# Recurrence of a one-core kernel: GpSimd computes two of VectorE's fp32 products in every time step

## The reference, cut to what matters

```python
def step(h, xs):
    xzt, xrt, xht = xs
    z = jax.nn.sigmoid(xzt + h @ U_z + vz)
    r = jax.nn.sigmoid(xrt + h @ U_r + vr)
    hh = jnp.tanh(xht + r * h @ U + vh)
    h_new = (1.0 - z) * h + z * hh
    return (h_new, h_new)
h0 = jnp.zeros((seq.shape[0], U.shape[0]), seq.dtype)
_, out_t = jax.lax.scan(step, h0, xs)
```

## Time and profile before

| what | value |
|---|---|
| median of 3 runs | 3793.93 us (3781.72 to 3805.06) |
| profiled execution | 3778.47 us |
| its span, first to last instruction | 3776.7 us |
| PE / DVE / ACT / POOL busy | 3250.4 / 2066.5 / 1501.4 / 628.7 us |
| one instruction of each of the 512 steps (ScalarE's r) | first at 2443.3 us, last at 3494.5 us |

### The profile page before, as it was taken

How to read it: one execution, slowest core, us unless ns; L and a number is a source line. 1 busy time by engine, 2 the same in 40 slices (tenths; PEclk the granted TensorE clock), 3 DMA queues, 4 the chain that set the end, 5 groups by cost and what they waited for, 6 DMA issues and landing times. The chain is left out here.

```text
span 3776.7 us, 109696 instructions
## 1 busy us (share of the span) xinstructions
PE 3250.4 (86%) x44394; PEld 2131.3 (56%) x44394; DVE 2066.5 (55%) x8157; ACT 1501.4 (40%) x4199; POOL 628.7 (17%) x361
## 2 busy tenths in 40 slices
PE   7895865899999876679986678899999999999899
PEld 3322442222333223678863234499999899999566
DVE  6324454555555515663327544377777677777554
ACT  3485541555454531666642222222222222222222
POOL 0000000666666750431110000000000000000000
PEclk8798987999999976899997789855555555555999
DMA  1000003000000005211110000100000000000000
GB/s 69 1 1 12 1 1 111 1 1 1 1 1 1 1 13 173 84 43 37 38 66 33 26 0 0 56 4 4 4 4 4 5 4 4 4 4 4 6 7 10
DMA packets 53379, 79.50 MB, mean 21 GB/s; under 512 B 11878, under 2 KB 43323, under 8 KB 51996
## 3 DMA queue, kind: packets, MB, share of 16 engines
q1 hardware_dynamic: 47504, 61.59, 4.9%
q0 software_dynamic: 3408, 9.34, 0.7%
q10 hardware_dynamic: 1988, 1.77, 0.2%
HBM read 56.01 MB, written 16.67 MB: 19 GB/s over the span
## 5 line engine op out<-in xcount | busy, mean ns | idle before, releaser
L1308 DVE TENSOR_REDUCE diff_mx<-diff_m_ps 128x1 f32<-128x512 f32 x512 | 330.0, 686 | 330.2 <-PE diff_m_ps L1158 330.2
L2756 PE MATMUL gru_sums<-gru_take,gru_u 128*128 128x4 f16 x12288 | 477.5, 167 | 5.5 <-issue 4.7
L2756 PE MATMUL gru_sums<-gru_keep,gru_u 128*128 128x4 f16 x12288 | 471.2, 166 | 4.1 <-DVE gru_keep L2830 2.2
L2756 PEld LDWEIGHTS gru_sums<-gru_take,gru_u 128*128 128x128 f16 x12288 | 430.4, 104 | 5.7 <-issue 4.8
L2756 PEld LDWEIGHTS gru_sums<-gru_keep,gru_u 128*128 128x128 f16 x12288 | 410.6, 104 | 18.3 <-issue 3.8
L1262 ACT ACTIVATE diff_probs<-diff_s_ps 128x512 f32<-128x512 f32 x512 | 277.9, 594 | 222.0 <-PE diff_s_ps L1152 221.9
L1152 PE MATMUL diff_s_ps<-diff_qk 32*128 32x512 f32 x1024 | 292.5, 645 | 63.6 <-DVE diff_mx L1308 56.0
L2756 PE MATMUL gru_sums<-gru_rh,gru_u 128*128 128x4 f16 x6144 | 280.1, 170 | 27.0 <-DVE gru_rh L2825 4.3
L1158 PE MATMUL diff_m_ps<-diff_qk 32*128 32x512 f32 x1024 | 293.6, 650 | 6.4 <-DVE diff_mx L1308 6.4
L1354 POOL TENSOR_TENSOR diff_sums<-diff_sums,diff_probs 128x2048 f32<-128x2048 f32 x64 | 289.4, 4521 | 31.4 <-ACT diff_probs L1262 31.1
L2756 PEld LDWEIGHTS gru_sums<-gru_rh,gru_u 128*128 128x128 f16 x6144 | 237.7, 107 | 69.4 <-DVE gru_rh L2825 6.0
(11 more groups left out here) (485 smaller groups left out, 5578.8 us busy)
## 6 DMA issues: line engine op xcount, KB each, us to landing
moe_weights<-in_L_ffn_W SPq DMA_DIRECT2D x16, 1024.0 KB, 12.8
expert_slots<-diff_blank SPq DMA_DIRECT2D x1, 5031.0 KB, 20.9
stream_a<-expert_slots SPq DMA_DIRECT2D x39, 129.0 KB, 2.1
moe_weights<-in_L_cond_w_R SPq DMA_DIRECT2D x1, 4096.0 KB, 15.4
moe_both<-expert_pairs SPq DMA_DIRECT2D x4, 1024.0 KB, 9.7
stream_b<-in_x SPq DMA_DIRECT2D x4, 512.0 KB, 8.1
hyp_wf<-in_L_cond_w_f SPq DMA_DIRECT2D x2, 1024.0 KB, 8.5
stream_b<-in_xT SPq DMA_DIRECT2D x1, 2048.0 KB, 12.2
```

The source lines that it names most:

```text
L1308: dve.tensor_reduce(mx[:, i % 2, kt, at:at + 1], m_ps[:, m % 3, :], X_AXIS, ALU.max).then_inc(ph.maxes_ready, 1)
L2756: last = pe.matmul(sums[:, par, g, m * B:(m + 1) * B], part[:, g, c, m * P:(m + 1) * P], state[:, c * B:(c + 1) * B], start=False, stop=(l ...
```

## The change

GpSimd gets a loop over the steps. In each it computes the fp32 `rh` = r*h and the fp32 `take` = hh*zs; VectorE no longer does. So that `take` is one plain product, VectorE computes `zs` = z times the scale, between `keep` and `keep2`. VectorE's `rh2` now waits for `rh1` and for `rh`, its `take2` for `take1` and for `take`. GpSimd's copies of the history stand between its products: three of four at the start of a step ahead of that step's `rh`, the fourth at the loop's end.

```diff
--- before.py
+++ after.py
@@ -2624,10 +2624,10 @@
         ph = Phase(nc, ctx, "gru")
         (ph.dve_step, ph.pe_done, ph.act_read, ph.h_ready, ph.r_sums, ph.z_sums, ph.hh_sums, ph.r_ready,
          ph.z_ready, ph.rh1_ready, ph.rh_ready, ph.rh2_ready, ph.keep1_ready, ph.keep_ready, ph.keep2_ready, ph.take1_ready,
-         ph.take_ready, ph.take2_ready, ph.hh_ready, ph.kept, ph.inputs_ready) = ph.semaphores(
+         ph.take_ready, ph.take2_ready, ph.hh_ready, ph.kept, ph.inputs_ready, ph.zs_ready) = ph.semaphores(
             "dve_step", "pe_done", "act_read", "h_ready", "r_sums", "z_sums", "hh_sums", "r_ready",
             "z_ready", "rh1_ready", "rh_ready", "rh2_ready", "keep1_ready", "keep_ready", "keep2_ready", "take1_ready",
-            "take_ready", "take2_ready", "hh_ready", "kept", "inputs_ready")
+            "take_ready", "take2_ready", "hh_ready", "kept", "inputs_ready", "zs_ready")
         N, KEPT, S = DC * B, KEPT_AT_ONCE, STEPS_IN_BODY
         COPIES = S // KEPT
         w, u, cw, bias, condT = early.w, early.u, early.cw, early.bias, early.condT
@@ -2648,6 +2648,7 @@
         r = ph.sb("r", [P, N])
         z = ph.sb("z", [P, N])
         rest = ph.sb("rest", [P, N])
+        zs = ph.sb("zs", [P, N])
         rh = ph.sb("rh", [P, N])
         rh1 = ph.sb("rh1", [P, N], F16)
         rh2 = ph.sb("rh2", [P, N], F16)
@@ -2823,12 +2824,14 @@
                         before = h[:, (s - 1) % S, :]
                         dve.wait_ge(ph.r_ready, t + 1)
                         dve.tensor_tensor(rh1[:, :], r[:, :], before, ALU.mult).then_inc(ph.rh1_ready, 1)
-                        dve.tensor_tensor(rh[:, :], r[:, :], before, ALU.mult).then_inc(ph.rh_ready, 1)
+                        dve.wait_ge(ph.rh1_ready, t + 1)
                         dve.wait_ge(ph.rh_ready, t + 1)
                         dve.tensor_tensor(rh2[:, :], rh[:, :], rh1[:, :], ALU.subtract).then_inc(ph.rh2_ready, 1)
                         dve.wait_ge(ph.z_ready, 2 * t + 1)
                         dve.tensor_tensor(keep1[:, :], rest[:, :], before, ALU.mult).then_inc(ph.keep1_ready, 1)
                         dve.tensor_tensor(keep[:, :], rest[:, :], before, ALU.mult).then_inc(ph.keep_ready, 1)
+                        dve.wait_ge(ph.z_ready, 2 * t + 2)
+                        dve.tensor_scalar(zs[:, :], z[:, :], SCALE, None, ALU.mult).then_inc(ph.zs_ready, 1)
                         dve.wait_ge(ph.keep_ready, t + 1)
                         dve.tensor_tensor(keep2[:, :], keep[:, :], keep1[:, :], ALU.subtract).then_inc(ph.keep2_ready, 1)
                         if s % KEPT == 0:
@@ -2836,8 +2839,7 @@
                         dve.wait_ge(ph.hh_ready, t + 1)
                         dve.scalar_tensor_tensor(out=take1[:, :], in0=hh[:, :], scalar=SCALE, in1=z[:, :], op0=ALU.mult,
                                                  op1=ALU.mult).then_inc(ph.take1_ready, 1)
-                        dve.scalar_tensor_tensor(out=take[:, :], in0=hh[:, :], scalar=SCALE, in1=z[:, :], op0=ALU.mult,
-                                                 op1=ALU.mult).then_inc(ph.take_ready, 1)
+                        dve.wait_ge(ph.take1_ready, t + 2)
                         dve.wait_ge(ph.take_ready, t + 1)
                         dve.tensor_tensor(take2[:, :], take[:, :], take1[:, :], ALU.subtract).then_inc(ph.take2_ready, 1)
                         dve.tensor_tensor(h[:, s, :], take[:, :], keep[:, :], ALU.add).then_inc(ph.h_ready, 1)
@@ -2849,12 +2851,23 @@
 
             @block.gpsimd
             def _(pool):
+                def keep_history(i, k):
+                    pool.tensor_copy(hist[:, :, bass.ds(S * i + k * KEPT, KEPT)],
+                                     h[:, k * KEPT:(k + 1) * KEPT, :].rearrange("p t n -> p n t")).then_inc(ph.kept, 1)
+
                 with pool.Fori(0, T // S) as i:
-                    for k in range(COPIES):
-                        pool.wait_ge(ph.h_ready, S * i + ((k + 1) * KEPT + 1))
-                        pool.tensor_copy(hist[:, :, bass.ds(S * i + k * KEPT, KEPT)],
-                                         h[:, k * KEPT:(k + 1) * KEPT, :].rearrange("p t n -> p n t")
-                                         ).then_inc(ph.kept, 1)
+                    for s in range(S):
+                        t = S * i + s
+                        pool.wait_ge(ph.h_ready, t + 1)
+                        if s and s % KEPT == 0:
+                            keep_history(i, s // KEPT - 1)
+                        pool.wait_ge(ph.r_ready, t + 1)
+                        pool.tensor_tensor(rh[:, :], r[:, :], h[:, (s - 1) % S, :], ALU.mult).then_inc(ph.rh_ready, 1)
+                        pool.wait_ge(ph.zs_ready, t + 1)
+                        pool.wait_ge(ph.hh_ready, t + 1)
+                        pool.tensor_tensor(take[:, :], hh[:, :], zs[:, :], ALU.mult).then_inc(ph.take_ready, 1)
+                    pool.wait_ge(ph.h_ready, S * i + (S + 1))
+                    keep_history(i, COPIES - 1)
         ph.rejoin()
```

## The result

| | before | changed |
|---|---|---|
| median | 3799.49 us (3781.72 to 3813.85, 4 runs) | 3959.94 us (3958.98 to 3961.63, 4 runs) |
| ratio to before | | 1.0411, 95% interval 1.0381 to 1.0441 |
| span of the profiled execution | 3776.7 us | 3959.9 us |
| recurrence, first to last r | 1051.2 us | 1201.3 us |
| median of the 511 distances between two r | 2.033 us | 2.307 us |

A forecast was written before the change was run, and what follows sets the result against it. The prediction took VectorE's second parts, `rh2` and `take2`, to be on the recurrence's circle. Their delays of 0.15 and 0.14 us a step, x 512, added 148 us to 3793.93: 3940 us, range 3865 to 4015.

The forecast's parts named there:

- The bound: Recurrence: TensorE waits 0.06 and 0.04 us for `rh2` and `take2`, so VectorE's second parts sit on the circle, 512 times.
- Item 1: Start of GpSimd's product behind r or `hh`: 0.15 us, 0.10 for the two-wait form plus 0.05 surplus over VectorE.
- Item 2: Duration of GpSimd's 128x8 product: 0.20 us, taken from copies of 2 columns, with bounds 0.07 and 0.61 us.
- Item 3: VectorE's second part, `rh2` or `take2`, starts 0.10 us behind GpSimd's end because it waits for two semaphores.
- The sum: Hand-over of 0.45 us against 0.30 (reset side) and 0.31 (new side): 0.29 us a step, 148 us in all.
- zs and the queues: `zs` fills a VectorE hole, work queued behind the waits shifts along: nothing; GpSimd's history copies 1 to 2 us, left out.
- The port: GpSimd's `rh` and `take` held until `rh1` and `take1` end, 0.05 us twice: +51 us, 3993 us; chance 0.13.
- (b): GpSimd's product takes twice VectorE's 0.16 us, 0.32 or more: +271 us or more, 4065 or more; chance 0.08.
- (c): GpSimd's product takes only 0.07 us, as the line through its long ones says: +15 us, 3809 us; chance 0.07.
- (d): GpSimd's product takes 0.07 us and an already satisfied second wait costs nothing: -51 us, 3743 us; chance 0.05.

The follow-up runs named there:

- e9: Changed kernel with the waits swapped as in e1, and t + 2 computed ahead of `keep2` so `take2` carries its wait for `take`: ratio to before 1.0031.
- e7: Kernel before with only `zs` added on VectorE between `keep` and `keep2`, read by nobody: step 2.033 us, recurrence 1048.2 us.
- e4: Kernel before, GpSimd untouched, with a second wait (`rh1`, `take1`) ahead of `rh2` and `take2`: ratio to before 1.021, step 2.167 us.
- e8: Kernel before with the fp32 product `keep` moved to GpSimd in place of the other two: ratio to before 1.0001, step 2.033 us.
- e5: Changed kernel with the two waits swapped on VectorE alone (`rh2`, `take2`): step 2.253 us, recurrence 1163.0 us.
- e6: Changed kernel with the two waits swapped on GpSimd alone, ahead of its two products: step 2.186 us, recurrence 1134.2 us.
- e1: Changed kernel with the two waits swapped ahead of `rh2`, `take2` and GpSimd's two products: ratio to before 1.0131, step 2.127 us.
- e12: Changed kernel with one more VectorE wait (for `keep1`) off the circle in each step: step 2.307 us, recurrence 1192.7 us.

## Why the prediction was right

*The bound.* It said that TensorE waits inside two blocks for second parts, so that every nanosecond there counts 512 times. Right, by the table's two columns: the step grows by what these two places grow by.

*Item 1, GpSimd's start.* 0.15 forecast, 0.142 measured; without the second wait 0.08 forecast, 0.076 in e9.

*Item 2, GpSimd's duration.* 0.20 forecast from the copies of 2 columns, 0.203 measured. The line through long products, which gave 0.07, misled by a factor of three: their cost per column says nothing of the fixed part. The factor of two over VectorE, as the Trainium skill has it (GPSIMD Engine Reference, section 3), gave 0.32 us, and the trace does not agree at this size: 0.203 against 0.160 us is 1.27.

*Item 3, VectorE's answer.* 0.10 forecast from the earlier trace rows, 0.104 measured.

*The sum.* 0.29 us a step forecast, 0.274 measured: 148 against 140 us. The term that was missing is the long steps, which gave 10 us more; without them the sum would have been 8 us too high, so the closeness of 148 to 150.1 is partly luck. The range 3865 to 4015 holds 3959.94; of its 18 us over the sum's 3942 only 2 are the recurrence's, 6 are the later median of the kernel before and the rest lies outside the recurrence.

*zs and the queues.* Costed at nothing; in e7 `zs` costs nothing. The copies of the history, left out at 1 to 2 us, make a step 0.6 us longer than its neighbours (2.92 to 2.95 against 2.307) where before it was 0.7 (2.73 to 2.76 against 2.033): no loss.

*The rivals.* The port: VectorE's `rh1` starts 0.033 us behind r and GpSimd's `rh` 0.142, and neither is longer than alone (0.168 and 0.203 us). In e9 GpSimd starts only about 0.04 us behind VectorE, and still neither grows in the common step. Once in 64 steps, where `take1` has two waits, e9 has GpSimd first by 0.03 us, and then VectorE's instruction takes 0.20 instead of 0.17 us:

```profile
3001.61 0.18 ACT L2803 ACTIVATE gru_hh<-gru_sums 128x8 f32<-128x8 f32 x1 [0.35 <-PE gru_sums L2757]
3001.87 0.20 POOL L2870 TENSOR_TENSOR gru_take<-gru_hh,gru_zs 128x8 f32<-128x8 f32 x1 [0.82 <-ACT gru_hh L2803]
3001.89 0.20 DVE L2841 SCALAR_TENSOR_TENSOR gru_take<-gru_hh,gru_z 128x8 f16<-128x8 f32 x1
```

So the lock that the Trainium skill describes (SBUF — State Buffer, Who interferes with whom) shows, as 0.03 us at eight places. It shows the other way round too, where GpSimd comes closer: four of e9's `rh` on GpSimd start 0.02 us behind `rh1` and take 0.217 instead of 0.201 us. Rivals (b) and (c) fall with the 0.203 us of item 2, and (d) with that and with e4, where a second wait whose first is up costs 0.07 us.

*What the prediction did not say.* Items 1 and 3 each have the price of a second wait in them, 0.10 instead of 0.03 us, but it took that form as given with the work and did not add the four up: 4 x 0.07 = 0.28 us, nearly its whole 0.29. With plain waits its own numbers give 0.08 + 0.20 + 0.03 = 0.31 us, what VectorE alone takes from r to `rh2` (0.311). e9 measures that. So the two products on GpSimd cost nothing and gain nothing in the common step; all of the common step's loss, 2 x (0.066 + 0.070) = 0.27 us, is the order in which two waits stand in the code. No rival asked what the other order would give.

## What to carry to other kernels

Where two waits stand ahead of one instruction, one becomes an instruction of the sequencer (here always the one coded second): let it be the one that is up first, let the late one be carried by the instruction itself, and see that no register instruction slips in between and takes it. Moving the second of two short instructions to another engine gained nothing here: the second engine's start, product and answer took 0.311 us, just what the one engine takes for both. And count the hand-over only if it is on the circle: e8 has the same kind of wait with room behind it and costs nothing.

## What the runs showed of the hardware

- A second wait that blocks the sequencer costs 0.066 us on GpSimd and 0.07 us on VectorE per use, although the other semaphore is up first (e5, e6; on VectorE without GpSimd's part 0.068 in e4); a register instruction that carries the wait costs 0.089 us (0.123 in e1 against 0.034 in e9).
- GpSimd's fp32 product of 128x8 takes 0.203 us, starts 0.076 us behind a ScalarE result, and VectorE follows 0.034 us behind its end.
- Every 128th instruction of VectorE's stream can come late, by 0.35 us directly behind an EVENT_SEMAPHORE (32 times in the changed kernel, 12 in e12). A stream of 16 instructions a step brings the place back to the same instruction every 8 steps, where it costs much (12.0 us in the changed kernel) or little (0.4 us in e7). The kernel before has it too, eight times 0.26 us at `keep1`.
- A product of VectorE or GpSimd that starts within 0.02 to 0.03 us behind the other engine's takes 0.02 to 0.03 us longer (e9: 0.20 instead of 0.17 and 0.217 instead of 0.201 us); a product of GpSimd 0.04 us behind does not.
